# A token convolution by one 512-token transform, or by two blocks of 256 tokens with three filters

## What is computed

```python
uv = silu(xn @ uv_w)
u, v = split(uv, 2, axis=-1)
a = concatenate([t_zero, t_pos, zeros((1, d)), t_neg], axis=0)   # t(k) * 0.99 ** |k|
y = irfft(rfft(a, n=2 * n, axis=0)[None] * rfft(v, n=2 * n, axis=1), n=2 * n, axis=1)
s = (u * y[:, :n]) @ o_w
...
h = gelu(einsum('nd,edf->enf', x_flat, W1) + b1[:, None, :])
expert_out = einsum('enf,efd->end', h, W2) + b2[:, None, :]
x = x + s * silu(layernorm(mixed_experts + xn) * gamma + beta)
```

## Time and profile before

| | us |
|---|---|
| median of 3 runs (lowest, highest) | 256.0 (255.84, 258.63) |
| the profiled execution, its own time | 255.08 |
| its span in the profile | 253.3 |
| TensorE busy | 233.1 (92%) |
| VectorE busy | 149.7 (59%) |
| ScalarE busy | 103.6 (41%) |

### The profile page before, as it was taken

How to read it: one execution, slowest core, us unless ns; L and a number is a source line. 1 busy time by engine, 2 the same in 40 slices (tenths; PEclk the granted TensorE clock), 3 DMA queues, 4 the chain that set the end, 5 groups by cost and what they waited for, 6 DMA issues and landing times.

```text
span 253.3 us, 3399 instructions
## 1 busy us (share of the span) xinstructions
PE 233.1 (92%) x1071; PEld 171.1 (68%) x1071; DVE 149.7 (59%) x467; ACT 103.6 (41%) x198; POOL 34.0 (13%) x53
## 2 busy tenths in 40 slices
PE   7989989799999999899999999999999999989823
PEld 6967546457666998479776777678776666756712
DVE  4655397735133436905465676877996786236484
ACT  1020757375274763961534233531334354223010
POOL 1830028211022002201000001001001001010100
PEclk9976999999599999999999999999999999999985
DMA  6143529723020750020342003200068100101002
GB/s 188 50 122 88 166 82 367 289 81 87 0 83 3 230 184 3 3 80 0 80 172 83 0 1 85 57 26 1 4 217 239 41 1 0 44 0 34 8 0 83
DMA packets 25154, 20.79 MB, mean 82 GB/s; under 512 B 1377, under 2 KB 22537, under 8 KB 24625
## 3 DMA queue, kind: packets, MB, share of 16 engines
q1 hardware_dynamic: 24608, 20.28, 25.9%
q10 hardware_dynamic: 528, 0.31, 0.6%
...
## 4 chain that ended last, share of the span: by engine, by line
PE 77%; DVE 8%; ACT 4%; issue 4%; DMA 4%; SPq 2%; POOLq 0%; ACTq 0%; POOL 0%; DVEq 0%
PE bank L1159 17%; PE bank L960 10%; PE bank L1191 10%; PE bank L961 9%; PE bank L962 9%; PE bank L957 6%; DMA w_raw<-in_L_ffn_W 4%; PE bank L1213 3%; PE bank L978 3%; PE bank L1058 3%; PE bank L1155 1%; PE bank L1092 1%; PE bank L1201 1%; ACT h_ring L523 1%; ACT yT L533 1%
## 5 line engine op out<-in xcount | busy, mean ns | idle before, releaser
L523 ACT ACTIVATE h_ring<-bank,b_sel 128x512 f32<-128x512 f32 x64 | 43.8, 688 | 60.7 <-PE bank L962 60.3
L1159 PE MATMUL bank<-h_ring,w_s 128*128 128x512 f32 x128 | 65.9, 599 | 0.0
L960 PE MATMUL bank<-xT_hi,w_hi 128*128 128x512 f32 x64 | 37.9, 593 | 1.7 <-ACT h_ring L523 1.6
L1191 PE MATMUL bank<-inv_sb,Y 128*128 128x256 f32 x128 | 29.0, 380 | 0.9 <-DVE conv L893 0.9
L1159 PEld LDWEIGHTS bank<-h_ring,w_s 128*128 128x128 f32 x128 | 24.4, 191 | 6.5 <-issue 1.0
L1191 PEld LDWEIGHTS bank<-inv_sb,Y 128*128 128x128 f32 x128 | 24.1, 190 | 6.4 <-issue 3.0
L961 PE MATMUL bank<-xT_lo,w_hi 128*128 128x512 f32 x64 | 25.7, 401 | 0.0
L962 PE MATMUL bank<-xT_hi,w_lo 128*128 128x512 f32 x64 | 25.7, 401 | 0.0
L610 POOL TENSOR_SCALAR root<-ymv 128x4 f32<-128x4 f32 x8 | 1.9, 238 | 132.8 <-DVE ymv L669 132.8
L960 PEld LDWEIGHTS bank<-xT_hi,w_hi 128*128 128x128 f32 x64 | 12.3, 193 | 10.3 <-issue 5.4
L957 PE MATMUL bank<-h_ring 128*128 128x256 f32 x44 | 16.0, 515 | 1.4 <-DVE h_ring L852 1.4
...
## 6 DMA issues: line engine op xcount, KB each, us to landing
x_ring<-in_L_attn_x SPq DMA_DIRECT2D x16, 256.0 KB, 3.3
w_raw<-in_L_ffn_W SPq DMA_DIRECT2D x16, 256.0 KB, 3.0
w_s<-in_L_ffn_W SPq DMA_DIRECT2D x16, 256.0 KB, 3.1
...
out_dram<-x_ring SPq DMA_DIRECT2D x8, 256.0 KB, 3.0
...
```

The lines of the kernel that those rows point to most:

```text
L523: nc.scalar.activation(h_ring[:, n % NH], H_PS[n % 2][:], ACT.Gelu, bias=b1_sel[b // GA][:, c, j, b % GA:b % GA + 1]).then_inc(h_done, 1)
L960: nc.tensor.matmul(out_ps, w_hi, m_hi, start=start, stop=False)
L1159: nc.tensor.matmul(OUT_PS[:], w2_s[:, b % 2, j, c], h_ring[:, n % NH], start=False, stop=(i == HT - 1)).then_inc(w2_mm, 1)
L1191: last = nc.tensor.matmul(EO_PS[:, ri * S // 2:(ri + 1) * S // 2], Y[:, kc, ri, b % GB], inv_sb[:, kc, ri], start=(kc == 0), stop=(kc == K ...
```

## The change

The 512 tokens are taken as two blocks (`NB`) of 256 (`H`). A transform has length 256 for a block and 2 frequency chunks (`KC`) in place of 4; the filter becomes three (own block, block before, block behind), which `A_sb` holds side by side. transform(q) now means chunk q // 2 mod 2 and block q mod 2: six matmuls in place of twelve. `products(q)` multiplies one block's transform by the two filters that lead to the two output blocks, so each instruction writes [128, 2, 4, 128], 1024 elements; for the second block it also adds to what the first left in `Y`. `spectrum` is gone as a job, since `products` does its sums. `transform_back` keeps eight matmuls, each 128 columns wide. The places in `FORTH_AT` and `BACK_AT` stay. `x_ring` holds all eight batches, so the second load falls away, and the tables are smaller (0.25 MB upper, lower and inverse, 1 MB lag) and loaded early.

```diff
-NC = S // 2 // P
-KC = S // P
-LC = S // P
+H = S // 2
+NB = S // H
+KC = H // P
+LC = H // P
+LAGS = 6
...
-SPECTRUM_AT = [25, 25, 26, 26]
+SPECTRUM_AT = [25, 26]
...
     ("products", 0): [n + 0.2 for n in FORTH_AT],
-    ("spectrum", 0): [n + 0.3 for n in FORTH_AT],
...
-        NX = NR = 4
+        NX = B
         x_ring = sb("x_ring", [P, NX, NT, D])
...
-        Y = sb("Y", [P, KC, 2, GB, D])
+        vt = sb("vt", [P, GB, 2, NB, D])
+        pm = sb("pm", [P, 2, 2, NB, D])
+        pm_hi = sb("pm_hi", [P, 2, NB, GB, D], F32R)
+        pm_lo = sb("pm_lo", [P, 2, NB, GB, D], F32R)
+        Y = sb("Y", [P, KC, 2, NB, GB, D])
         prod = sb("prod", [P, 4, GB, D])
-        A_sb = sb("A_sb", [P, KC, 2, D])
-        cs_hi = sb("cs_hi", [P, NC, 2, S], F32R)
...
-                    sp.wait_ge(xsum_ps, n - NX + 1)
-                sp.dma_start(x_ring[:, n % NX], x_v[n]).then_inc(x_in[n % NX], 16)
-
-            def reload_x(b):
...
             sp.dma_start(uvw, uv_w).then_inc(uvw_in, 16)
-            load_x(GA)
+            for dst, src in ((cs_raw[:, 0], t_upper), (cs_raw[:, 1], t_lower)):
+                sp.dma_start(dst, src).then_inc(cs_in, 16)
+            for b in range(GA, B):
+                load_x(b)
 
...
 
             fetch_w1(0)
             fetch_w2(0)
-            load_x(GA + 1)
+            sp.dma_start(lag_flat, t_lag).then_inc(lag_in, 16)
+            sp.dma_start(inv_sb[:].rearrange("p a r i -> p (a r i)"), t_inv).then_inc(inv_in, 16)
             fetch_w1(1)
             fetch_w2(1)
-            load_x(GA + 2)
-            load_x(GA + 3)
-            sp.dma_start(cs_raw, t_upper).then_inc(cs_in, 16)
-            sp.dma_start(Y[:].rearrange("p a r b d -> p (a r b d)"), t_lag).then_inc(lag_in, 16)
             for dst, src in ((ow_sb[:], o_w), (gam[:], gamma.partition_broadcast(P)),
...
                 act_e.wait_ge(cs_in, 32)
-                nc.scalar.activation(cs_lo[:, c].rearrange("p r k -> p (r k)"),
-                                     cs_raw[:, c * 2 * S:(c + 1) * 2 * S], ACT.Copy).then_inc(cs_lo_done, 1)
+                for n, dst in enumerate((cs_hi, cs_lo)):
+                    nc.scalar.activation(dst[:].rearrange("p r k -> p (r k)"), cs_raw[:, n],
+                                         ACT.Copy).then_inc(cs_done, 1)
...
-                    nc.scalar.activation(teto[:, n].rearrange("p q d -> p (q d)"),
-                                         A_PS[n][:], ACT.Copy).then_inc(teto_done, 1)
+                nc.scalar.activation(teto[:, 0, 0], A_PS[0][:, 0:D], ACT.Copy, scale=half0).then_inc(teto_done, 1)
+                nc.scalar.activation(teto[:, 0, 1:4].rearrange("p q d -> p (q d)"), A_PS[0][:, D:4 * D],
+                                     ACT.Copy).then_inc(teto_done, 1)
+                nc.scalar.activation(teto[:, 1, 0:4].rearrange("p q d -> p (q d)"), A_PS[2][:],
+                                     ACT.Copy).then_inc(teto_done, 1)
+                nc.scalar.activation(teto[:, :, 4:6].rearrange("p l q d -> p l (q d)"),
+                                     A_PS[1][:].rearrange("p (l w) -> p l w", l=LC),
+                                     ACT.Copy).then_inc(teto_done, 1)
 
             def filter_read():
 
                 act_e.wait_ge(A_ps, 1)
-                for m in range(2):
-                    nc.scalar.activation(A_sb[:, 2 * m:2 * m + 2].rearrange("p a r d -> p (a r d)"),
-                                         A_PS[m][:], ACT.Copy).then_inc(A_done, 1)
+                for kc in range(KC):
+                    for ri in range(2):
+                        src = A_PS[2 * kc + ri]
+                        nc.scalar.activation(A_sb[:, kc, ri, 1], src[:, 0:D], ACT.Copy)
+                        nc.scalar.activation(A_sb[:, kc, ri, 0], src[:, D:2 * D], ACT.Copy,
+                                             scale=1.0 if ri == 0 else -1.0)
+                        nc.scalar.activation(A_sb[:, kc, ri, 2], src[:, 2 * D:3 * D],
+                                             ACT.Copy).then_inc(A_done, 1)
 
             def gelu(n):
...
             def products(q):
 
-                kc = q % KC
-                a_re = bcast(A_sb[:, kc, 0].unsqueeze(1), [P, GB, D])
-                a_im = bcast(A_sb[:, kc, 1].unsqueeze(1), [P, GB, D])
-                v_re = V_RI[0][:].rearrange("p (b d) -> p b d", b=GB)
-                v_im = V_RI[1][:].rearrange("p (b d) -> p b d", b=GB)
+                kc, s = q // NB % KC, q % NB
+                lo = NB - 1 - s
+                a_re, a_im = (bcast(A_sb[:, kc, ri, lo:lo + NB].unsqueeze(2), [P, NB, GB, D]) for ri in range(2))
+                v_re, v_im = (bcast(V_RI[ri][:].rearrange("p (b d) -> p b d", b=GB).unsqueeze(1), [P, NB, GB, D])
+                              for ri in range(2))
+                y_re, y_im = Y[:, kc, 0], Y[:, kc, 1]
                 if q == 0:
-                    dve.wait_ge(A_done, 2)
+                    dve.wait_ge(A_done, 2 * KC)
+                if q == KC * NB:
+                    dve.wait_ge(eo_ps, GB)
                 if q >= 1:
                     dve.wait_ge(Y_done, q)
                 dve.wait_ge(vre_ps, q + 1)
-                nc.vector.tensor_tensor(prod[:, 0], v_re, a_re, ALU.mult)
-                nc.vector.tensor_tensor(prod[:, 1], v_re, a_im, ALU.mult).then_inc(vre_read, 1)
+                if s == 0:
+                    nc.vector.tensor_tensor(y_re, v_re, a_re, ALU.mult)
+                    nc.vector.tensor_tensor(y_im, v_re, a_im, ALU.mult).then_inc(vre_read, 1)
+                else:
+                    nc.vector.tensor_tensor(part[0], v_re, a_re, ALU.mult)
+                    nc.vector.tensor_tensor(part[1], v_re, a_im, ALU.mult).then_inc(vre_read, 1)
+                    dve.wait_ge(vre_read, q + 1)
+                    nc.vector.tensor_tensor(y_re, y_re, part[0], ALU.add)
+                    step(nc.vector.tensor_tensor(y_im, y_im, part[1], ALU.add))
                 dve.wait_ge(vim_ps, q + 1)
-                nc.vector.tensor_tensor(prod[:, 2], v_im, a_im, ALU.mult)
-                nc.vector.tensor_tensor(prod[:, 3], v_im, a_re, ALU.mult).then_inc(vim_read, 1)
+                nc.vector.tensor_tensor(part[0], v_im, a_im, ALU.mult)
+                nc.vector.tensor_tensor(part[1], v_im, a_re, ALU.mult).then_inc(vim_read, 1)
+                dve.wait_ge(vim_read, q + 1)
+                nc.vector.tensor_tensor(y_re, y_re, part[0], ALU.subtract)
+                nc.vector.tensor_tensor(y_im, y_im, part[1], ALU.add).then_inc(Y_done, 1)
...
-                for cc in range(2):
-                    last = nc.tensor.matmul(A_PS[cc][:], act[:, cc * P:(cc + 1) * P],
-                                            ow_v.rearrange("p q d -> p (q d)"), start=True, stop=True)
+                for cc in range(LC):
+                    nc.tensor.matmul(A_PS[2 * cc][:], act[:, cc * P:(cc + 1) * P],
+                                     ow_v[:, 0:4].rearrange("p q d -> p (q d)"), start=True, stop=True)
+                    last = nc.tensor.matmul(A_PS[1][:, cc * 2 * D:(cc + 1) * 2 * D], act[:, cc * P:(cc + 1) * P],
+                                            ow_v[:, 4:6].rearrange("p q d -> p (q d)"), start=True, stop=True)
                 last.then_inc(teto_ps, 1)
 
             def filter_spectrum(kc):
 
                 if kc == 0:
-                    pe.wait_ge(teto_done, 2)
+                    pe.wait_ge(teto_done, 4)
                     pe.wait_ge(lag_in, 16)
+                col = slice(kc * P, (kc + 1) * P)
                 for ri in range(2):
-                    o = (kc % 2) * 2 * D + ri * D
+                    ps = A_PS[2 * kc + ri]
                     for lc in range(LC):
-                        last = nc.tensor.matmul(A_PS[kc // 2][:, o:o + D],
-                                                lag_sb[:, lc, ri, kc * P:(kc + 1) * P],
-                                                teto[:, lc % 2, 2 * (lc // 2) + ri],
-                                                start=(lc == 0), stop=(lc == LC - 1))
+                        nc.tensor.matmul(ps[:, 0:D], lag_sb[:, lc, ri, col], teto[:, lc, ri],
+                                         start=(lc == 0), stop=(lc == LC - 1))
+                    for near in range(2):
+                        for lc in range(LC):
+                            last = nc.tensor.matmul(ps[:, D:3 * D], lag_sb[:, lc, ri + 2 * near, col],
+                                                    teto[:, lc, 4 - 2 * near:6 - 2 * near].rearrange("p q d -> p (q d)"),
+                                                    start=(near == 0 and lc == 0),
+                                                    stop=(near == 1 and lc == LC - 1))
                 if kc == KC - 1:
...
             def transform(q):
 
-                kc = q % KC
+                kc, s = q // NB % KC, q % NB
                 if q == 0:
-                    pe.wait_ge(cs_lo_done, 2)
-                    pe.wait_ge(A_done, 2)
-                if kc == 0:
```

(27 more changed lines are left out.)

159 lines of the change are left out of this document (69 added, 90 removed).

## The result

The changed kernel takes 273.2 us, median of 4 runs (271.43 to 273.44), where the kernel before takes 255.9 (255.44 to 258.63) beside it. The ratio is 1.064, 95% interval 1.055 to 1.072: slower, by 17 us. The prediction was 278.0, range 268 to 287. The profiled execution took 273.03 us, its span is 271.2 and its mean granted clock 0.907 (before 0.956).

What follows compares the result with a forecast made beforehand. VectorE's products were taken to bound both groups. The terms 1.8 + 9.8 - 4.9 + 15.4 - 5.0 made 17.1 us, with the clock 22.1, on the profiled 255.1: 277.2, or 278 on the runs' scale, range 268 to 287.

Steps and rivals of the forecast that it cites:

- The products: On VectorE: a 1024-element instruction is 1.23 us long at a pitch of 1.13; four transforms of a group take 33 us.
- The first group: From transform(0) to transform_back(0): VectorE's products stretch 24.5 us to 34.3, +9.8, and TensorE waits for `Y_done`.
- The second group and the end: Second group to transform_back(4): +15.4, 41.6 us in place of 26.2; afterwards three shorter ways back on the path, -5.0.
- Between the groups: From transform_back(0) to the second group's first product: -4.9 us, as VectorE's waits for the way back's odd part nearly vanish.
- The clock: TensorE's clock falls to half behind its idle times before transform_back(0) and `hidden(56)`: 2.5 us each, 5.0 in all.
- Ahead of transform(0): Before the first transform: +1.8 us from lags, spectrum and filter copies, less table copies and a wait of 0.47 us.
- 0.86 + 1.55 + 0.3 - 0.4: Before transform(0): lag matmuls +0.86, spectrum +1.55, ScalarE's filter copies +0.3, fewer table copies -0.4 us.
- (2): Rival: the products bound the kernel, but the clock costs nothing: 273 us; chance 20%.
- (4): Rival: the clock also falls inside the groups, TensorE late by up to 4 us twice more: 286 us; chance 12%.
- (1): Rival: a wide VectorE instruction costs what a narrow one does, so products hide behind TensorE: 235 us; chance 3%.
- (5): Rival: VectorE's chain hides more, by overlapping sums or less idle time in the middle: 262 to 267 us; chance 8%.
- (3): Rival: the early transfers also hold up the first weights: +2, 280 us; chance 8%.

Runs made afterwards that it cites:

- e1_half_products: The changed kernel with each VectorE product and sum making one output block in place of two, half the convolution's output left out: 245.1 us, ratio 0.960.
- e2_busy: The changed kernel with 32 idle TensorE matmuls ahead of its wait before transform_back(0) and 10 ahead of the wait before hidden(56): 272.7 us, ratio 1.067.
- e4_places: The changed kernel with other places in the tables that set the order, no work added or taken away: 260.1 us, median of 11 runs.
- e6_places_busy: The changed kernel with other places in the order tables, plus 34 idle TensorE matmuls ahead of the wait before transform_back(0): 259.4 us, ratio 1.019.

## Why the prediction was right, and where it was off

The mechanism is as forecast: VectorE's products set the length of both groups, and the loss comes from these two stretches (+9.8 and +15.8). Of the 4.2 us by which the sum is too high in the profile (22.1 against 17.9), 2.5 are a fall of the clock that costs nothing, and 1.7 stand ahead of transform(0). Slips inside the sum are small: the wait on an own result is 0.12 and not 0.11, 22.7 less 14.8 is 7.9, and 39.8 and a unit of 1.56 make 41.4.

**The products.** An instruction of 1024 elements takes 1.22 us at a pitch of 1.13 to 1.14, taken as 1.23 and 1.13. The first group is 33.1 us of VectorE (33 predicted), and its stretch 34.6 (34.3). This was the step on which all hung, and half products undo it.

**The second group and the end.** The lower weights end 39.5 us behind the first product (39.8 predicted). The two stretches together changed by +10.64 us against +10.4 without the clock, and the cut of 5.0 at the end came out as 5.13. Part of this is luck. At full clock (e2_busy) the second group is 40.6 us, +14.3, and the end 41.5, only -3.7. From one way back to the next the end then changes by -0.2, -1.7 and -1.7 us: the first of the three shorter ways back is hidden behind the same wait for `yT` as the second fall. The term for the group was 1.1 too long and the cut at the end 1.3 too large, and these errors cancel.

**Between the groups.** Without the clock's 2.35 us it is -5.0 (-4.9 predicted). VectorE's waits for the odd part went from 5.2 us to 2.1 (1.16 and 0.90), and in e2_busy, where the first way back is at full clock, to 0.23. So they nearly vanish, as forecast, and what was left of them belongs to the fall of the clock.

**The clock, 5.0 us: half of it wrong.** The fall behind transform_back(0) costs 2.35 us (idle matmuls), as sized. For the one behind `hidden(56)` I wrote that TensorE is the path behind it. It is not: `norm` on VectorE, tanh and `yT` on ScalarE arrive no sooner. That term is 0 in place of 2.5, and is the larger mistake. I had looked for VectorE's wait behind each fall and not for ScalarE's queue. The idle time ahead of `hidden(56)` was off too, 2.54 us and not 6 to 10: TensorE stood earlier in the group as well, 3.82 us for a bank at 205.22 and 4.38 for a gelu at 219.18. That gelu stood on ScalarE behind a tanh that waited for VectorE's `norm` (until 217.92), which the prediction didn't follow.

**Ahead of transform(0), +1.8: measured +0.13.** The filter's own matmuls hold. TensorE's timeline of the kernel after, from the places that tell the difference:

```profile
36.80 1.42 PE L963 MATMUL bank<-xT_hi,w_hi 128*128 128x512 f32 x1
...
62.19 3.63 PE L981 MATMUL bank<-rstd,x_ring 128*128 128x1 f32 x32
...
102.03 0.50 PE L963 MATMUL bank<-xT_hi,w_hi 128*128 128x512 f32 x1 [1.08 <-ACT h_ring L525]
```

and of the kernel before at two of them:

```profile
61.02 4.22 PE L978 MATMUL bank<-rstd,x_ring 128*128 128x1 f32 x32
65.11 0.77 PE L960 MATMUL bank<-xT_hi,w_hi 128*128 128x512 f32 x1
...
103.88 0.50 PE L960 MATMUL bank<-xT_hi,w_hi 128*128 128x512 f32 x1 [1.09 <-ACT h_ring L523]
```

From the unit at 102.03 (103.88 before) to transform(0) it is 21.22 us against 19.24: +1.98 for lags, spectrum and copies, which I had as 0.86 + 1.55 + 0.3 - 0.4 = 2.31. The 0.3 for the copies is nothing: transform(0) starts without a wait. The first copy of 128 columns takes 0.28 us, as the line gave, the mean is 323 ns, and all twelve are done in 2.15 us, from 120.74 to 122.89. The wait of 0.47 us is gone too. But ahead of it the clock fell elsewhere: before, `mean_rows` and the units behind it ran at half clock from 63.9 to 70.6; after, they did not (3.63 in place of 4.22 us, and full speed behind), while the units from 36.5 to 40 did. Net that gave 1.4 us back, which no term of mine held. It is no merit of the change: in four other profiles with the same instructions up to there (e1_half_products, e2_busy, e4_places, e6_places_busy) transform(0) starts at 124.8 to 127.5 us.

**The rivals.** (2) names the measured time, 273, and is half true: one of two falls costs nothing. That the number fits is luck, since the other fall cost 2.35 us and the stretch ahead of transform(0) came out 1.7 too short. (4) is true in its first half: the clock fell inside both groups (0.88 and 0.80 on average) and TensorE waited; but the end of each group stayed VectorE's, which has no wait from 189.05 to 229.75. (1) is out by the rows, (5) by the pitch and by the -5.0 between the groups. (3): TensorE's wait at 16 us is the same 0.90 in both kernels and its first expert unit starts at the same time to 0.1, so the early transfers of x, 6.4 us from issue to landing in place of 3.3, held up nobody.
